# VectorE in place of GpSimd for one addition per half-batch in the first two layers of a transformer stack, and the following statistics one slot earlier

## The reference, cut to what matters

```python
x = x + L0_xattn(layernorm(x), ctx)      # 16 heads over 77 context rows
x = x + L0_ffn(layernorm(x))             # the spline layer, below
x = x + L1_xattn(layernorm(x), ctx)      # next norm: statistics "c" in the kernel
...
# in L0_ffn, on its normalised input xf:
y = xf + mag * directions[tile_idx] * output_scale[0]
y = (y - mean(y)) / sqrt(var(y) + eps) * norm_gamma + norm_beta
```

## Time and profile before

| what | value |
|---|---|
| Median of 3 runs | 2973.98 us (2966.57 to 2975.74) |
| The profiled execution's own time | 2977.86 us |
| Its span in the profile | 2976.1 us |
| DVE busy over the span | 1962.4 us (66%) |
| PE, ACT, POOL busy | 81%, 51%, 27% |
| Span of the stage with the change | from about 55 us to about 800 us |

### The profile page before, as it was taken

The page is one execution under the profiler, slowest core; times in us unless marked ns, Lnnn a source line. Parts: engine busy times, 40 slices in busy tenths (PEclk is TensorE's granted clock), DMA queues, the critical chain, the costliest instruction groups (busy, mean ns, idle before and its releaser), DMA issues. The chain is left out here.

```text
span 2976.1 us, 43560 instructions
## 1 busy us (share of the span) xinstructions
PE 2417.7 (81%) x16502; PEld 1975.3 (66%) x16502; DVE 1962.4 (66%) x4449; ACT 1508.6 (51%) x2566; POOL 809.2 (27%) x707
## 2 busy tenths in 40 slices
PE   4778888877589999999849999999999276767665
PEld 3545554544477887888739999999999255555544
DVE  4688878875556666666526566666664468686867
ACT  2456667653445665565425444444543255545443
POOL 2233434432222433444440000000000572626030
PEclk9788888886699999999969999999999698988887
DMA  7500000000100111100014334333441511211000
GB/s 234 208 1 16 15 1 15 8 8 15 38 1 1 44 35 38 36 20 15 20 66 134 118 124 140 127 117 118 139 134 57 166 47 35 63 33 57 1 15 15
DMA packets 152616, 184.22 MB, mean 62 GB/s; under 512 B 21560, under 2 KB 118101, under 8 KB 152408
## 3 DMA queue, kind: packets, MB, share of 16 engines
q1 hardware_dynamic: 139400, 154.16, 15.8%
q0 software_dynamic: 12288, 27.15, 2.9%
q10 hardware_dynamic: 720, 0.12, 0.0%
HBM read 116.38 MB, written 71.43 MB: 63 GB/s over the span
## 5 line engine op out<-in xcount | busy, mean ns | idle before, releaser
L2355 POOL DMA_INDIRECT picked<-expert_out,so x128 | 126.8, 990 | 866.3 <-DMA so<-slots 765.1
L157 PE MATMUL SC<-Xhi,Whi 128*128 128x320 f32 x1024 | 319.9, 312 | 7.1 <-DVE Wlo L2148 5.3
L157 PE MATMUL SC<-Xlo,Whi 128*128 128x320 f32 x1024 | 316.9, 310 | 0.0
L157 PE MATMUL SC<-Xhi,Wlo 128*128 128x320 f32 x1024 | 316.9, 309 | 0.0
L631 POOL TENSOR_TENSOR PR<-PR,rs 128x616 f32<-128x616 f32 x128 | 157.8, 1233 | 410.0 <-DVE rs L1014 410.0
L1384 POOL TENSOR_TENSOR ff_Hlo<-ff_HF,ff_Hhi 128x512 fp32r<-128x512 f32 x112 | 148.0, 1322 | 419.4 <-ACT ff_Hhi L1517 419.3
L2125 ACT ACTIVATE Hhi<-HF 128x320 fp32r<-128x320 f32 x256 | 120.7, 471 | 154.7 <-DVE HF L2178 154.7
L157 PEld LDWEIGHTS SC<-Xhi,Whi 128*128 128x128 f32 x1024 | 193.0, 188 | 7.8 <-DVE Wlo L2148 5.7
L2167 DVE TENSOR_TENSOR Hlo<-HF,Hhi 128x320 fp32r<-128x320 f32 x256 | 125.5, 490 | 104.3 <-ACT Hhi L2125 104.3
L2148 DVE TENSOR_TENSOR Wlo<-Wraw,Whi 128x1024 fp32r<-128x1024 f32 x96 | 114.6, 1223 | 119.2 <-ACT Whi L2113 119.2
L157 PEld LDWEIGHTS SC<-Xlo,Whi 128*128 128x128 f32 x1024 | 193.1, 189 | 0.0
(11 more groups left out here) (477 smaller groups left out, 6979.4 us busy)
## 6 DMA issues: line engine op xcount, KB each, us to landing
expert_in<-zeros SPq DMA_DIRECT2D x4, 5120.0 KB, 32.7
rowsin<-expert_in SPq DMA_DIRECT2D x32, 640.0 KB, 6.0
expert_out<-rowsout SPq DMA_DIRECT2D x32, 640.0 KB, 4.0
Wraw<-L_wg SPq DMA_DIRECT2D x32, 512.0 KB, 7.0
Wraw<-L_wu SPq DMA_DIRECT2D x32, 512.0 KB, 7.2
Wraw<-L_wd SPq DMA_DIRECT2D x32, 512.0 KB, 7.9
X<-x SPq DMA_DIRECT2D x8, 512.0 KB, 4.3
x_after_l_attention<-X SPq DMA_DIRECT2D x8, 512.0 KB, 2.8
```

The source lines that it names most:

```text
L157: last = nc.tensor.matmul(out, lhs[l], rhs[r], start=start and n == 0, stop=stop and n == 2)
L2355: nc.gpsimd.indirect_dma_start(picked[g][:, t, k, :], None, oute[:, :], bass.IndirectOffsetOnAxis(ap=so[g][:, t, k:k + 1], axis=0)).then_i ...
```

## The change

`add_spline` moves from POOL's list to DVE's, still in slot 14, and the statistics "c" move from slot 15 to slot 14, behind it. Nothing is computed otherwise.

```diff
@@ -635,12 +635,6 @@
                         x = X[h % NXA][:, :, :]
                         nc.gpsimd.tensor_tensor(x, x, bc_at(row[:, :], 1, TT), add).then_inc(done, 1)
 
-                    def add_spline(h):
-                        pool.wait_ge(scaled_g, h + 1)
-                        x = X[h % NXA][:, :, :]
-                        pool.wait_ge(beta_added, h + 1)
-                        nc.gpsimd.tensor_tensor(x, x, XN[h % G][:, :, :], add).then_inc(x2_ready, 1)
-
                     def keys0(b):
                         pool.wait_ge(kcol_ready, b + 1)
                         if b:
@@ -686,8 +680,6 @@
                                 add_row(p, bo0r, xn_p, bias0_added)
                             if s == (10 if p == 0 else 12) and p < NH and p % G == 0:
                                 values0(p // G)
-                            if s == 14 and 0 <= c1 < NH:
-                                add_spline(c1)
                             if s == 15 and 0 <= h < NH:
                                 add_row(h, betar, xn_a, beta_added)
 
@@ -1101,6 +1093,12 @@
                         xn = XN[h % G][:, :, :]
                         tt(xn, xn, bc_at(gammar[:, :], 1, TT), ALU.mult).then_inc(scaled_g, 1)
 
+                    def add_spline(h):
+                        dve.wait_ge(scaled_g, h + 1)
+                        dve.wait_ge(beta_added, h + 1)
+                        x = X[h % NXA][:, :, :]
+                        tt(x, x, XN[h % G][:, :, :], ALU.add).then_inc(x2_ready, 1)
+
                     def add_first(h):
                         dve.wait_ge(y0_psum, h + 1)
                         dve.wait_ge(bias0_added, h + 1)
@@ -1176,7 +1174,9 @@
                                 ln_rstd(h, LN["a"], var_a, sd_a, rstd_a)
                             if s == 13 and 0 <= c1 < NH:
                                 scale_by_gamma(c1)
-                            if s == 15 and 0 <= c1 < NH:
+                            if s == 14 and 0 <= c1 < NH:
+                                add_spline(c1)
+                            if s == 14 and 0 <= c1 < NH:
                                 dve.wait_ge(x2_ready, c1 + 1)
                                 ln_stats(X[c1 % NXA], LN["c"], var_c)
                     dve.wait_ge(x_done, NH)
```

## The result

The changed kernel takes 2980.30 us (2973.74 to 2984.04, 12 runs), the kernel before, timed beside it, 2971.67 us (2965.05 to 2978.26, 12 runs): a ratio of 1.0027, 95% interval 1.0015 to 1.0038. By the medians that is +8.6 us; 7.8 were forecast. The bound of 0.3% lies inside the interval, so it is no difference by that bound, at its slow edge. Timed again later it gave 1.0032 (1.0018 to 1.0045).

The account below looks back on a forecast made before the run. DVE was taken to be near its limit, busy 70.3 of 80 us. Five periods' 7.3 us plus 0.5 for the seventh half-batch gave +7.8 on the median 2973.98: 2981.8 us, range 2971 to 2991.

Parts of the forecast that it names:

- Part 1: Addition on DVE in slot 14: 1.21 us, about 1.14 us added to DVE's list, eight times: +9.1 us.
- the bound from above: DVE's addition takes up to 1.21 + 1.23 us if it must let a POOL instruction finish first.
- Part 2: DVE no longer waits for POOL's addition (x2_ready): -9.8 us over the eight half-batches.
- Part 3: Addition and statistics put unit 15's shift 2.96 us later, delaying PE's queue and sd_c: +1.46 us for the period.
- 1.46 us for all five: Second to sixth half-batch: unit 17's shift starts 1.46 us later in each, 7.3 us together.
- the bounds: Limits on the +7.8 us sum: 4 from below, 9.9 without L1029's gift, up to 12 with PE's lower clock.
- which nobody waits for: Unit 13's normalisation on POOL ends at 325.1 instead of 324.2, harmless while unit 16's scores wait until 327.4.
- The seventh and the last half-batch: Seventh: unit 14's PT starts later, +0.5 us; last: sd_c's table load starts as before, 0.
- The draw: Shrinking waits for sd_a or sd_g absorb the later sd_c, leaving DVE's account at -0.7 us (2973.3); chance 0.22.
- a sign of being wrong: Waits for sd_a and sd_g shrinking in the changed kernel's profile would show the forecast wrong; no size given.
- The lost lock: POOL's normalisation starts first, DVE's addition waits 1.39 us more in six half-batches: +16.1 us (2990); chance 0.14.
- POOL's list on the path: POOL's 18.9 us saved all count, against DVE's 9.1: 9.8 us faster (2964); chance 0.06.

Follow-up runs that it names:

- n_before: Kernel before without the square root of norm c on ScalarE (variance used instead, so different results): 2964.60 us, 0.9990 of the kernel before.
- w2_pool_a_slot_earlier: Kernel before with the addition still on POOL but in slot 13 instead of 14: 2962.59 us, 0.9978 of the kernel before.
- e2_stats_only: Kernel before with only the statistics moved to slot 14, addition still on POOL: 2998.77 us, 1.0107 of the kernel before.
- e1_add_only: Changed kernel with the statistics back in slot 15, so only the addition moves to DVE: 2972.11 us, 1.0012 of the kernel before.
- f_pe_filled: Changed kernel with unit 13's five transposes done three times in slot 15 to fill PE's gap: 2972.96 us, 1.0021 of the kernel before.
- e9_add_behind_gamma: Changed kernel with DVE's addition in slot 13 behind gamma and statistics in slot 15: 2978.20 us, 1.0031 of the kernel before.
- e3_both_late: Changed kernel with addition and statistics both on DVE in slot 15 instead of 14: 2973.18 us, 1.0023 of the kernel before.

## Why the prediction was right, and where it was not

**The total and the direction** were right: +7.8 us forecast, +8.6 by the medians, +8.3 at the end of the stage in the profiled executions. But 8.3 is made of larger parts: +0.5 ahead of the second gamma (in fact ahead of the first, where nothing differs), +12.5 in the five slot times, -2.8 in the rest of those periods and -1.9 behind the seventh gamma. I had 7.3, 0 and +0.5 for the last three. A price too small and a giving back left out cancelled each other, so the closeness of the total is partly luck.

**Part 1, the addition.** It takes 1.18 to 1.19 us where DVE is first, 1.31 in the mean of eight; the bound from above shows up in the last half-batch, 2.12 us. 1.21 was the right value to take, 0.8 us too little over the eight.

**Part 2, the wait for POOL** is gone to the last microsecond, 9.8 us. By itself such a wait was worth little: without the 10.1 us of waits for `sd_c` the stage of n_before is 3.2 us shorter, and with 3.9 us less of waits for X the slot times of w2_pool_a_slot_earlier together 1.3 us.

**Part 3, the place ahead of unit 15's shift**, was the heart, and its chain is confirmed up to the scores. In the third period, with 0.23 us added for the later start of the addition, the forecast puts the shift of 15 at 326.03 (measured 326.01) and the scores at 327.7 (327.75). In the context periods `rstd_c` came 1.59 us later against gamma (1.56 forecast) and the slot time grew by 1.49 and 1.51 us (1.46 forecast). e2_stats_only shows by the dose that the place has a price. Not confirmed is that `sd_c` is the door by which all of it comes: without the root the stage is still 7.6 us longer. And the waits for `sd_c` were not near 2.4 us in all five periods but 1.4, 3.8, 1.4, 3.8 and 3.2.

**The step that was mis-sized** is 1.46 us for all five: in three periods it was 3.57, 3.57 and 2.37. In the third the forecast chain, 0.23 us later, has the norm transposes at 328.98; they started at 330.09, 1.11 us late, because scores and values ran at the lower clock. XT stood 2.01 us behind them instead of 1.13, 0.88 more. With 0.15 behind that it makes 2.14 us. Of these, 1.4 show in the wait of `rstd_c`, 3.82 rather than 2.4 us; the rest is a wait that I had at nothing, since DVE was to reach the shift of unit 16 "as today" and waited 0.64 us for its scores. I had the lower clock in the bounds, at 0.79 us a period for the scores alone; values and transposes pay it too, and in the sixth period only the transposes do.

**The sentence that does not hold** is that POOL's longer normalisation is one "which nobody waits for". DVE was first, by 0.16 us instead of 0.13, and POOL's instruction took 2.10 us, both as forecast. But PE waits for it, with unit 13's transposes. I only asked when their result is needed, and it is indeed not needed earlier; I did not ask what PE's clock does when it stands idle. Nor did I ask it of the second gap, the 1.62 us ahead of the scores, which is in the forecast itself: there the scores wait for the late shift. e1_add_only has the first gap alone, and its scores are slow in two periods of three; f_pe_filled leaves the first, fills the second and is fast in one of three; e9_add_behind_gamma has other gaps and no collision and is slow. Together they tie the lower clock to idle time of PE; which gap does it in which period stays open.

**The seventh and the last half-batch.** From gamma to `rstd_c` the seventh grew from 13.21 to 14.67 us, 1.5 instead of 0.5; there too PE's norm transposes took 1.97 us instead of 1.10. The last shrank from 8.91 to 7.92 (0 forecast).

**The rivals.** The draw's reason, that `sd_a` and `sd_g` wait less, is real in part, 2.5 us of 12.9. The prediction had named that shrinking as a sign of being wrong; it came, and was too small to make a draw. The lost lock happened in the last half-batch only (timeline of DVE):

```profile
723.38 2.12 DVE L1100 TENSOR_TENSOR X<-X,XN 128x1024 f32<-128x1024 f32 x1
```

There POOL's normalisation had been blocked by gamma and held the addition back in turn. POOL's list on the path: the 12.7 us that POOL saved brought nothing.

## What to carry to other kernels

Between engines that feed each other through ordered lists, price a moved instruction by what is queued behind its new place on every engine, and a removed wait by what is late next: here 9.8 us of waits went and 12.9 came back elsewhere, and the place ahead of the shift cost 1.5 us a time at the full clock and up to 3.6 where the clock fell. Before writing that nobody waits for a lengthened instruction, check whether it leaves TensorE without work, since the matmuls behind the gap may then run at the lower clock. Closing one door (the queue's head, the root) is no proof of a gain: here the wait came back at another. If an addition must be out of the way, look first for an idle stretch of the engine that already does it.

## What the runs showed of the hardware

- DVE and POOL hold each other up where both work on SBUF operands: the normalisation went from 1.23 to 2.10 us behind DVE's addition, the addition from 1.18 to 2.12 behind the normalisation, POOL's beta addition from 2.36 to 3.34 (e3_both_late), and a DVE instruction on 128x4 elements from 0.16 to 1.07 (n_before). The delay shows as a longer instruction, not as idle time before it.
- The clock of PE fell to 1.2 GHz for some microseconds behind gaps of 1.54 and 1.62 us with 0.77 us of work between them, behind a single 1.76 us gap (e1_add_only, third and sixth period), and behind 2.00 and 0.88 us (e9_add_behind_gamma). It did not behind 1.61 us where PE had been busy ahead (context periods), nor behind 1.76 us in the fifth period of e1_add_only and of f_pe_filled. So the length of a gap alone does not tell.
- At the lower clock the same matmuls took 1.40 instead of 0.79 us, 1.08 instead of 0.64, and 1.97 instead of 1.09: 1.7 to 1.8 times as long.
